# Latent attention: where ACT copies a finished group's output, between a slot's two exponentials or behind them

## The reference

```python
q = (x @ Wq).reshape(b, t, H, D).transpose(0, 2, 1, 3)        # H = 16, D = 64
ckv = x @ Wkva                                                # latent of 32, rotary key of 32
kv_latent, k_rope = (ckv[:, :, :R], ckv[:, :, R:])
kv = (kv_latent @ Wkvb).reshape(b, t, H, NOPE).transpose(0, 2, 1, 3)
...
att = jnp.einsum('bhqd,bhkd->bhqk', q, k) / jnp.sqrt(jnp.float32(D))
att = jnp.where(mask, att, jnp.float32(-jnp.inf))             # mask: lower triangle
att = jax.nn.softmax(att, axis=-1)
y = jnp.einsum('bhqk,bhkd->bhqd', att, v)
return y.transpose(0, 2, 1, 3).reshape(b, t, H * D) @ Wo
```

## Time and profile before

| | |
|---|---|
| timed runs | 2958.74 us median of 3 (2956.3 to 2959.84) |
| profiled execution, its own time | 2952.6 us |
| its span | 2950.8 us |
| TensorE busy in the span | 2521.9 us (85%) |
| VectorE, ACT, POOL busy | 1762.0, 1274.5, 807.6 us |
| latent attention, units | about 560 to 1690 us |
| the copy L1497 | 128 times, 596 ns in the mean |

### The profile page before, as it was taken

One profiled execution on the slowest core, in us unless ns is written; L12 is line 12 of the kernel. 1 busy time (PEld: TensorE's weight loads), 2 busy tenths in 40 slices (PEclk: granted clock), 3 DMA queues, 4 the chain that ended last, 5 costly groups with the idle time before them and its releaser, 6 DMA issues. The chain is left out here.

```text
span 2950.8 us, 44249 instructions
## 1 busy us (share of the span) xinstructions
PE 2521.9 (85%) x16472; PEld 2002.7 (68%) x16472; DVE 1762.0 (60%) x3013; ACT 1274.5 (43%) x1879; POOL 807.6 (27%) x934
## 2 busy tenths in 40 slices
PE   4699973799999999999999759999567875999998
PEld 4577752567777777777777548888344544788887
DVE  3488772477667766776677456565323335576564
ACT  0566651366565665566666523332122223323322
POOL 0123223244434343534333211121223432000100
PEclk8799995799999999999999879999788986999999
DMA  2301102333334333333333140100100003000000
GB/s 107 100 27 46 31 18 68 102 115 102 92 109 124 104 99 109 112 94 100 111 106 107 41 145 8 46 31 15 63 31 30 9 22 120 8 24 8 31 8 15
DMA packets 126955, 194.62 MB, mean 66 GB/s; under 512 B 34592, under 2 KB 92960, under 8 KB 122080
## 3 DMA queue, kind: packets, MB, share of 16 engines
q1 hardware_dynamic: 124960, 191.40, 21.4%
q10 hardware_dynamic: 1792, 0.53, 0.1%
HBM read 118.44 MB, written 61.34 MB: 61 GB/s over the span
## 5 line engine op out<-in xcount | busy, mean ns | idle before, releaser
L1255 DVE TENSOR_REDUCE l_negmax<-l_mx 128x1 f32<-128x512 f32 (+3 forms) x608 | 394.3, 654 | 146.1 <-PE l_mx L1604 145.5
L1485 ACT ACTIVATE l_Phi<-l_s 128x1024 fp32r<-128x1024 f32 x288 | 295.0, 1024 | 264.9 <-PE l_s L1624 256.7
L1267 DVE TENSOR_TENSOR l_Plo<-l_s,l_Phi 128x1024 fp32r<-128x1024 f32 x288 | 349.9, 1215 | 13.5 <-ACT l_s L1489 12.8
L1635 PE MATMUL l_o<-l_Phi,l_V 128*128 128x256 f32 x1152 | 308.9, 290 | 7.1 <-ACT l_Osb L1497 2.7
L1622 PE MATMUL l_s<-l_QA,l_KK 128*128 128x512 f32 x576 | 284.6, 494 | 26.4 <-DVE l_Plo L1267 23.6
L2259 ACT ACTIVATE m_hidhi<-m_h 128x512 fp32r<-128x512 f32 x168 | 106.2, 632 | 458.4 <-DVE m_h L2117 458.4
L1635 PE MATMUL l_o<-l_Plo,l_V 128*128 128x256 f32 x1152 | 302.2, 284 | 0.0
L1604 PE MATMUL l_mx<-l_KK,l_QA 128*128 128x512 f32 (+3 forms) x768 | 274.7, 398 | 26.3 <-DMA l_QB<-l_qd 14.6
L1489 ACT ACTIVATE l_s<-l_s 128x1024 f32<-128x1024 f32 x288 | 295.3, 1025 | 0.0
L1635 PEld LDWEIGHTS l_o<-l_Phi,l_V 128*128 128x128 f32 x1152 | 221.5, 192 | 43.1 <-issue 31.7
L1624 PE MATMUL l_s<-l_QB,l_KL 65*128 65x512 f32 x576 | 231.1, 401 | 0.0
(11 more groups left out here) (346 smaller groups left out, 5932.9 us busy)
## 6 DMA issues: line engine op xcount, KB each, us to landing
l_qd<-l_qs SPq DMA_DIRECT2D x256, 128.0 KB, 2.4
l_QA<-l_qd SPq DMA_DIRECT2D x64, 512.0 KB, 4.4
l_QB<-l_qd SPq DMA_DIRECT2D x64, 256.0 KB, 5.2
l_R<-l_rd SPq DMA_DIRECT2D x128, 128.0 KB, 3.0
l_rps<-l_rp SPq DMA_DIRECT2D x128, 64.0 KB, 1.9
m_xb<-xs SPq DMA_DIRECT2D x8, 1024.0 KB, 4.8
w_xb<-in_x SPq DMA_DIRECT2D x4, 1024.0 KB, 6.8
w_Vodd<-w_V SPq DMA_DIRECT2D x8, 512.0 KB, 5.3
```

The lines of the kernel that those rows point to most:

```text
L1255: v.tensor_reduce(negmax[:, n % 2, at + h0:at + h1], piece_of(number, chunk), AX.X, ALU.max, negate=True).then_inc(reduced, 1)
L1267: v.tensor_tensor(Plo[:, s % 3].rearrange("p u h q -> p (u h q)"), S2[s % 2][:, :], Phi[:, s % 3].rearrange("p u h q -> p (u h q)").bitcas ...
L1485: a.activation(Phi[:, s % 3].rearrange("p u h q -> p (u h q)"), S2[s % 2][:, :], ACT.Exp, scale=L_D ** -0.5).then_inc(exped, 1)
L1635: mm = pe.matmul(O[:, odd * 2 * P:(odd + 1) * 2 * P].rearrange("p (j q) -> p j q", j=2), V[:, b % 2, k, 64 - 64 * odd:192 - 64 * odd], src ...
```

## The change

In an iteration that both closes a slot (u odd) and copies a group, ACT ran first exponential, copy, second exponential. Now it runs first exponential, second exponential, copy. An iteration without a copy, or with even u, is as before.

```diff
                 group = L.evacuated(u)
                 if L.is_step(m) and u % 2 == 1:
                     exp_high(u // 2)
+                if L.is_step(m) and u % 2 == 1:
+                    exp_full(u // 2)
                 if group is not None:
                     evacuate(group)
-                if L.is_step(m) and u % 2 == 1:
-                    exp_full(u // 2)
                 if i == 1 and L.is_step(m + 3):
                     query_high(m + 3)
```

## The result

The changed kernel takes 2992.66 us (median of 4 runs, 2984.36 to 2996.47) where the kernel before took 2957.52 (4 runs, 2954.27 to 2959.84). The ratio is 1.0116, with a 95% interval from 1.0090 to 1.0142: 35.1 us slower. The forecast was 2990.

A forecast was written before the change was run, and what follows sets the result against it. TensorE bounds the kernel, and the copy already gates it, just barely. Added waits of 41.6 us less 10.3 given back make +31.3 on the profiled 2952.6, so 2983.9, carried to the median 2990 us; range 2973 to 3006.

The forecast's parts named there:

- 49 places, 41.6 us: Odd-slot copies in the latent attention: the later copy makes TensorE wait longer at 49 places, 41.6 us in sum.
- the 30 copies: Copies right behind the first exponential, no slack behind them: each 0.91 to 0.94 us later, 27.6 us.
- the 8 and 11: 8 copies at i = 4, 0.84 us each, 6.7 us; 11 in between, 0.46 to 0.80 each, 7.3 us.
- 14 free ones: Moved copies to cost nothing: 11 with long TensorE work behind them, 3 that wait about 4 us for the weighing.
- Given back, 10.3 us: Later TensorE waits in the phase that shrink after the added stalls: 10.3 us, bounds zero and 24.7.
- directly behind the moved pairs: TensorE's 13 waits of about 0.2 us for the subtraction behind moved pairs go: 2.1 us given back.
- Part (a): Six waits for the DMA of the maximum row, where the moved copy stands at i = 4, give back 2.7 us.
- Part (b): Three waits of 3.6 to 3.8 us for a row maximum lose 0.2 to 0.6 each, 1.2 us.
- (c): Five or six TensorE waits behind an overfull VectorE lose up to one stall each, 4.3 us.
- "The exponential was the gate": Rival: the later copy costs nothing, the earlier second exponential helps; 2956 us, at best 2946; chance 0.05, mixture 0.03.
- "The clock falls": Rival: added stalls drop TensorE's matmuls to 1.2 GHz, 20 us more, 3010 us; chance 0.14 of more than 3002.
- "More is absorbed": Rival: the phase's waits absorb the full 24.7 us, +17, 2976 us; chance 0.13 for a gain back beyond 18.

The follow-up runs named there:

- the 19 alone: Against the kernel before, only the 8 copies at i = 4 and the 11 in between moved behind the second exponential: +3.0 us, run again +1.7 us.
- second trace of before: The unchanged kernel before, executed once more for its trace: 2953.18 us.
- both_late: Against the kernel before, a stand-in exponential of the same size ahead of the copy in 63 odd slots, so copy and second exponential are late: +36.1 us.

## Why the prediction was right

- **49 places, 41.6 us.** The 49 intervals grew by 28.0 + 14.2 = 42.2 us, those of the 30 copies by 28.0 against 27.6, the 8 and 11 by 14.2 against 14.0. In the changed kernel the weight load follows the copy's end by 0.11 at all 49. The 14 free ones gained 0.1 here and -2.8 us alone, not told from zero.
- **TensorE does not make it good.** Right for the whole. In the 19 alone the times show 2 to 3 us of 14 left, and the intervals from score to score 6 to 7: half of this class's stall comes back within the step.
- **Given back, 10.3 us.** The right order of size with the wrong parts. The rest of the phase gave 7.2 back (-18.0 and +10.7 in places), and a second trace of before differs from the first by +2.2 there, so this is known to a few microseconds. The term "directly behind the moved pairs", 2.1 us for 13 waits of 0.2, was sized too small: these intervals shrank by 7.4 us, in 21 places, since the idle time that the list gives a matmul is only a part of what a wait costs. Part (a), 2.7 us, showed in part: TensorE's waits for the row of maxima fell from 4.1 us in 8 places to 2.3 in 3. Part (b), 1.2 us, did not show: the three long waits for a row maximum are 3.46, 3.97 and 3.73 us where they were 3.78, 3.61 and 3.79 (3.81, 5.30 and 3.51 in the second trace of before). Nor did (c), 4.3 us: of the five waits behind a full VectorE the three that were 1.3 are 1.8, 1.9 and 1.8, and the two of 1.6 have stayed. Why those three grew is open.
- **Net +31.3, time 2990.** TensorE's idle time in the phase rose by 31.3; 3.7 us more of busy time stand beside it. That the first agrees to the tenth is luck, given the scatter, and since the parts of the 10.3 were off in both directions. The measured +35.1 us has an interval of 26.6 to 42.0.
- **"The exponential was the gate"** fell: an exponential half a microsecond earlier left VectorE's wait for it at 12.6 us (12.8 before), and one that was 0.9 us later than before (both_late) made the phase 6.4 us longer than the changed kernel's, in one trace each, where the copy's lateness costs 35.
- **"The clock falls"** did not decide. 54 weighings at the lower level against 47 and 36 in two traces of before is within what before does by itself. They are not spread over the 49 places. In each of the nine traces of before, the changed kernel, both_late and the kernels with a part of the copies moved, 24 to 32 of them stand in the same iterations (39 to 41, 183 to 185, 327 to 329), right behind the three long waits for a row maximum. These waits are 3.2 to 5.3 us in the nine traces, and the clock fell around the end of all 27: in before they end at 627.02, 915.16 and 1201.48, and the granted clock is 0.5 from 627.5 to 634.4, from 914.2 to 921.1 and from 1201.0 to 1207.8. Behind shorter waits it fell now and then. The stretch at 1286.43 is in that trace of before; the second trace of before has the same wait, 1.32 us up to 1285.00, and no slow weighings behind it, and so has the changed kernel with 1.82 us. But another of the changed kernel's waits of 1.8 us, up to 722.25, was followed by the lower level.
- **"More is absorbed"** fell for the whole at +35.1. But its mechanism is real: it is the 7.4 us above, for which this rival named the same waits, those for the subtraction. Of it 5.1 us stand behind the 19 and only 2.3 behind the 30.
- **A rule on the weight load.** In the changed kernel the load starts at 605.68, 0.11 behind the copy's end, and the matmul 0.04 later. So the load was not pulled ahead over the wait, and none of its 0.19 us lay inside. The Trainium skill (TensorE: Matmul & The Clock Gate, Architectural detail: the array is 16x 32x32, not 1x 128x128) says that TensorE can pull a weight load ahead of matmuls in flight. Here the 9.3 us that the prediction worked out by it did not come off.

Not tried: a second output tile. The Trainium skill (Perfetto Trace Analysis, Optimizing Tensor Performance, Matmuls) advises to rotate independent groups through different PSUM banks, so that one's evacuation overlaps the next one's matmuls. No run here shows what that would give: the phase's PSUM tiles already come to eight of 128x512, and something else would have to go for a ninth. Open too: why the number of slow matmuls differs between executions, worth some 15 us of busy time between these traces (1062.9 to 1077.8 in the kernels with some copies moved).

## What to carry to other kernels

An in-order engine with room in the mean can still hold the gate at one instruction. Look at the weight load, not only at the matmul: a constant 0.11 us between the end of a copy and the next load, at place after place, marks a gate without slack, even where the list of waits shows 2.7 us for it. Then price a later copy at its full delay times the number of such places, and take off what the next waits behind them give back, measured from one score to the next, since a matmul's listed idle time is only a part of its wait. Before covering the gate with other work, look which ring is the next to be full.

## What the runs showed of the hardware

- A semaphore from ACT to TensorE's weight load shows as 0.11 or 0.12 us, and the load's wait as "issue": 75.0 us in the changed kernel, of which the matmuls' list names 37.7.
- A wait can cost more than the idle time listed at its matmul. At 583.02 the list has 0.20 us, and the interval from score to score is 0.36 us longer than without the wait (1.54 against 1.18).
- A stall is partly paid back by the next wait that does not depend on it: 0.34 to 0.40 us behind each of eight stalls of about 0.85, the same in every trace in which they occur.
- Around the end of each of 27 waits of TensorE of 3.2 to 5.3 us (three in each of nine traces) the granted clock fell to 0.5. Behind the same wait of 1.3 us (up to 1285.28 and 1285.00) it fell in one trace of before and not in the other.
- Two traces of the same kernel, before, differ by 2.7 us in this phase and have 47 and 36 slow weighings.
